# Taking four means over features from the sum of two chunks: the additions on GpSimd and VectorE

## The reference, cut to what matters

```
x = x + a_alpha * attention(gamma * rms(x) + beta)        # 16 heads; rms: x * rsqrt(mean(x*x) + eps)
x = x + f_alpha * swiglu(gamma * rms(x) + beta)           # hidden 1024
h = x * scale * rsqrt(mean(x*x) + eps)                    # MLP with gelu, 8-bit rounding of its hidden values
x = y + x
x = x + up(relu(down(x) + bd)) + bu                       # adapter, width 128, weights made per batch
x = (x - mean(x)) * rsqrt(var(x) + eps) * weight + ...    # layer norm
```

## Time and profile before

| | us |
|---|---|
| median of 3 runs | 1082.66 (1082.04 to 1083.32) |
| the profiled execution | 1081.34 |
| its span, first to last instruction | 1079.5 |
| PE busy | 996.1 |
| DVE busy | 749.6 |
| ACT busy | 552.4 |
| POOL busy | 194.8 |

### The profile page before, as it was taken

The page is one execution under the profiler, slowest core; times in us unless marked ns, Lnnn a source line. Parts: engine busy times, 40 slices in busy tenths (PEclk is TensorE's granted clock), DMA queues, the critical chain, the costliest instruction groups (busy, mean ns, idle before and its releaser), DMA issues.

```text
span 1079.5 us, 22413 instructions
## 1 busy us (share of the span) xinstructions
PE 996.1 (92%) x7426; PEld 846.0 (78%) x7426; DVE 749.6 (69%) x1711; ACT 552.4 (51%) x1160; POOL 194.8 (18%) x250
## 2 busy tenths in 40 slices
PE   5586999999999999999999999999999999998965
PEld 4244769798988979797989889797979898896952
DVE  3735468786777877786867778777868677776552
ACT  3163464656555564646565555646465655545430
POOL 1411421111120202021111202020211112020210
PEclk9576989999999999999999999999999999999995
DMA  8984543040403022130404030221304040300000
GB/s 287 292 326 130 203 148 89 2 138 2 138 1 118 20 74 63 40 98 1 137 1 137 1 117 20 74 63 40 98 1 137 1 137 1 117 13 20 2 20 10
DMA packets 78049, 89.45 MB, mean 83 GB/s; under 512 B 18672, under 2 KB 64640, under 8 KB 75392
## 3 DMA queue, kind: packets, MB, share of 16 engines
q1 hardware_dynamic: 72368, 63.86, 19.9%
q0 software_dynamic: 2304, 16.78, 4.2%
q10 hardware_dynamic: 3344, 8.39, 2.3%
HBM read 63.14 MB, written 25.31 MB: 82 GB/s over the span
## 4 chain that ended last, share of the span: by engine, by line
PE 74%; issue 10%; DVE 5%; DMA 4%; ACT 3%; POOL 2%; SPq 2%; ACTq 0%; DVEq 0%; POOLq 0%
PE bank L648 15%; PE bank L603 14%; PE bank L617 7%; PE bank L572 6%; PE bank L562 5%; PE bank L546 5%; PE bank L520 5%; PE bank L506 3%; PE bank L666 3%; PE bank L529 2%; ACT probs L877 2%; PE bank L680 2%; PE bank L686 1%; PE bank L589 1%; PE bank L627 1%
## 5 line engine op out<-in xcount | busy, mean ns | idle before, releaser
L463 POOL TENSOR_TENSOR act_lo<-act_f,act_hi 128x256 fp32r<-128x256 f32 x128 | 95.9, 755 | 414.4 <-ACT act_hi L920 414.4
L877 ACT ACTIVATE probs<-bank 128x512 f32<-128x512 f32 x256 | 139.6, 599 | 54.7 <-PE bank L562 53.9
L1132 DVE TENSOR_REDUCE neg_max<-bank 128x2 f32<-128x512 f32 x256 | 162.0, 682 | 0.4 <-PE bank L546 0.4
L914 ACT ACTIVATE silu_g<-bank 128x256 f32<-128x256 f32 x128 | 49.2, 385 | 190.2 <-PE bank L603 190.0
L956 ACT ACTIVATE gelu_g<-bank,r 128x256 f32<-128x256 f32 x128 | 60.8, 475 | 95.6 <-PE bank L648 94.8
L562 PE MATMUL bank<-q_stack,k_stack 128*128 128x256 f32 x512 | 98.5, 315 | 12.1 <-ACT probs L877 11.8
L648 PE MATMUL bank<-up_hi,h_hi 128*128 128x256 f32 x512 | 108.1, 293 | 1.6 <-DVE y L1105 1.0
L603 PE MATMUL bank<-h_hi,gh_hi 128*128 128x256 f32 x512 | 103.6, 284 | 4.6 <-DVE h_lo L1193 4.6
L603 PE MATMUL bank<-h_lo,gh_hi 128*128 128x256 f32 x512 | 103.3, 283 | 0.0
L603 PE MATMUL bank<-h_hi,gh_lo 128*128 128x256 f32 x512 | 103.0, 283 | 0.0
L648 PE MATMUL bank<-up_lo,h_hi 128*128 128x256 f32 x512 | 102.9, 282 | 0.0
(11 more groups left out here) (160 smaller groups left out, 2131.8 us busy)
## 6 DMA issues: line engine op xcount, KB each, us to landing
hyper<-w_hyper POOLq DMA_DIRECT2D x16, 1024.0 KB, 6.7
q_stack<-q_dram SPq DMA_DIRECT2D x96, 128.0 KB
k_stack<-k_dram SPq DMA_DIRECT2D x96, 128.0 KB
q_dram<-probs SPq DMA_DIRECT2D x16, 512.0 KB, 2.8
k_dram<-probs SPq DMA_DIRECT2D x16, 512.0 KB, 3.6
x_res<-xT SPq DMA_DIRECT2D x16, 256.0 KB, 2.8
out<-xc SPq DMA_DIRECT2D x16, 256.0 KB, 2.5
x_in<-xT SPq DMA_DIRECT2D x15, 256.0 KB, 2.7
```

The lines of the kernel that those rows point to most:

```text
L463: pool.tensor_tensor(act_lo[:, c % 3, :], act_f[:, c % 2, :], act_hi[:, c % 3, :].bitcast(F32), ALU.subtract).then_inc(g_lo.sem, 1)
L877: act.activation(probs[:, h % SLOTS], halves(SCORE_BANKS[h % 3]), ACT.Exp, scale=float(H / D) ** 0.5).then_inc(s_exp.sem, 1)
L1132: dve.tensor_reduce(neg_max[:, qt, :, pair:pair + 1].rearrange("p a o -> p (a o)"), halves(n % 3), AX_X, ALU.max, negate=True).then_inc(ma ...
```

## The change

Each of the five means but the norm of batches 0 and 1 ahead of attention is now taken of the sum of the two chunks, so the product with mean_w has one chunk. New functions make the sum, in place or in a tile that is free: on GpSimd sum_a (n1, after the sixth act_lo), sum_x and sum_square_x (n4, ahead of layer_out); on VectorE sum_g (n3, between norm_a(nxt) and scaled_y(g)) and sum_f (n2, after residual_1). New semaphores n1_sum to n4_sum tell TensorE. On TensorE project_v(nxt, 1) moves from behind norm_f to ahead of ln_var, and norm_f waits once for the sum in place of once for each chunk. project_v(nxt, 0) for a run without a is dropped; no run has nxt without a.

```diff
+                def sum_a(b):
+                    pool.wait_ge(n1_act.sem, n1_act.at(b, 1))
+                    pool.tensor_tensor(h1[:, 0, :], h1[:, 0, :], h1[:, 1, :], ALU.add).then_inc(n1_sum.sem, 1)
+                def sum_x(b):
+                    pool.wait_ge(x4_dve.sem, x4_dve.at(b))
+                    pool.tensor_tensor(adapt_h[:], x3[:, 0, :], x3[:, 1, :], ALU.add).then_inc(n4_sum.sem, 1)
+                def sum_square_x(b):
+                    pool.wait_ge(n4_act.sem, n4_act.at(b, 1))
+                    pool.tensor_tensor(sq4[:, 0, :], sq4[:, 0, :], sq4[:, 1, :], ALU.add).then_inc(n4_sum.sem, 1)
...
+                            if nxt and c == 5:
+                                sum_a(nxt)
...
+                        sum_x(g)
+                        sum_square_x(g)
                         layer_out(g)
...
+                def mean_of_sum(at, total):
+                    return pe.matmul(at, mean_w[:], total, start=True, stop=True)
...
+                        pe.wait_ge(n1_sum.sem, n1_sum.at(b, back=2))
+                        mean_of_sum(bank[4][:, 0:T], h1[:, 0, :]).then_inc(n1_pe.sem, 1)
...
-                    for c in range(DC):
-                        pe.wait_ge(n2_act.sem, n2_act.at(b, c + 1))
-                        mm = pe.matmul(bank[4][:, 0:T], mean_w[:], h2[:, c, :], start=(c == 0), stop=(c == DC - 1))
-                    mm.then_inc(n2_pe.sem, 1)
+                    pe.wait_ge(n2_sum.sem, n2_sum.at(b))
+                    mean_of_sum(bank[4][:, 0:T], h2[:, 0, :]).then_inc(n2_pe.sem, 1)
...
-                    pe.wait_ge(n3_act.sem, n3_act.at(b, 1))
+                    pe.wait_ge(n3_sum.sem, n3_sum.at(b))
                     for t in range(TT):
-                        for c in range(DC):
-                            mm = pe.matmul(bank[3][:, t:t + 1], sq3[:, c, t * P:(t + 1) * P], mean_w[:, 0:1],
-                                           start=(c == 0), stop=(c == DC - 1))
+                        mm = pe.matmul(bank[3][:, t:t + 1], sq3[:, 0, t * P:(t + 1) * P], mean_w[:, 0:1], start=True, stop=True)
...
-                    pe.wait_ge(x4_dve.sem, x4_dve.at(b))
-                    mean(bank[7][:, 0:T], x3).then_inc(n4_pe.sem, 1)
+                    pe.wait_ge(n4_sum.sem, n4_sum.at(b, 1))
+                    mean_of_sum(bank[7][:, 0:T], adapt_h[:]).then_inc(n4_pe.sem, 1)
...
-                    pe.wait_ge(n4_act.sem, n4_act.at(b, 1))
-                    mean(bank[6][:, 0:T], sq4).then_inc(n4_pe.sem, 1)
+                    pe.wait_ge(n4_sum.sem, n4_sum.at(b, 2))
+                    mean_of_sum(bank[6][:, 0:T], sq4[:, 0, :]).then_inc(n4_pe.sem, 1)
...
-                            norm_a(nxt)
+                            norm_a(nxt, summed=f is not None)
...
+                    if nxt:
+                        project_v(nxt, 1)
                     if g:
                         ln_var(g)
-                    if nxt and not a:
-                        project_v(nxt, 0)
                     if a:
                         norm_f(a)
-                    if nxt:
-                        project_v(nxt, 1)
...
+                def sum_g(b):
+                    dve.wait_ge(n3_act.sem, n3_act.at(b, 1))
+                    dve.tensor_tensor(sq3[:, 0, :], sq3[:, 0, :], sq3[:, 1, :], ALU.add).then_inc(n3_sum.sem, 1)
+                def sum_f(b):
+                    dve.wait_ge(n2_act.sem, n2_act.at(b, DC))
+                    dve.tensor_tensor(h2[:, 0, :], h2[:, 0, :], h2[:, 1, :], ALU.add).then_inc(n2_sum.sem, 1)
...
                     if nxt:
                         norm_a(nxt)
+                    if f:
+                        sum_g(f)
                     if g:
                         scaled_y(g)
...
                         residual_1(a)
+                        sum_f(a)
                     if g:
                         layer_norm(g)
```

More of the change, by code:

```diff
@@ L244, in build @@
         den_act, o_dve = sem("den_act", 4), sem("o_dve", 16)
+        n1_sum, n2_sum, n3_sum, n4_sum = sem("n1_sum"), sem("n2_sum"), sem("n3_sum"), sem("n4_sum", 2)
         wo_mm, x1_dve, x1_bias = sem("wo_mm", DC), sem("x1_dve", 2), sem("x1_bias", DC)
@@ L507, in mean, with norm_a @@
                     return mm
-                def norm_a(b):
+                def mean_of_sum(at, total):
+                    return pe.matmul(at, mean_w[:], total, start=True, stop=True)
+                def norm_a(b, summed=False):
                     pe.wait_ge(n1_act.sem, n1_act.at(b, 1))
-                    mean(bank[4][:, 0:T], h1).then_inc(n1_pe.sem, 1)
+                    if summed:
+                        pe.wait_ge(n1_sum.sem, n1_sum.at(b, back=2))
+                        mean_of_sum(bank[4][:, 0:T], h1[:, 0, :]).then_inc(n1_pe.sem, 1)
+                    else:
+                        mean(bank[4][:, 0:T], h1).then_inc(n1_pe.sem, 1)
                 def project_qk(b):
```

## The result

The changed kernel takes 1100.05 us (median of 4, 1097.32 to 1109.02) against 1082.56 (1082.04 to 1083.32; a fourth execution has joined the three above): ratio 1.0175, 95% interval 1.0117 to 1.0234, slower by 17.5 us. The forecast was 1099. The profiled execution took 1100.66 (span 1098.5). Three executions of the experiments ran in a slow state (two of the eighth at 1869 us, one of the sixth at 1139 us) and are in no ratio.

What follows compares the result with a forecast made beforehand. PE, busy 92%, was taken to set the pace. Thirteen full runs +9.4, end runs +1.4 and +1.1, run 1 +4.4 sum to +16.3 us; on 1081.34 that is 1097.6, with the median 1.3 above, 1099; range 1090 to 1108.

Steps and rivals of the forecast that it cites:

- norm_a, 0.0 us: At norm_a, POOL's sum_a is free, but its gain is hidden because ffn_out waits for act_lo: 0.0 us per full run.
- norm_g, +0.87 us: At norm_g, PE stands 1.3 us for sum_g, queued on DVE behind residual_2 and norm_a: +0.87 us per full run.
- Tail, -0.15 us: From ln_mean to the up projection, sum_f eats ln_mean's gain and gated_u(1) holds the fourth up piece: -0.15 us per run.
- the 0.17 us: In the tail, gated_u(0)'s wait for DVE's Newton steps, which come earlier, is taken out: 0.17 us.
- The stated waits: In the tail: ln_mean waits little or not for POOL, ln_var within 0.3 us; guess_f's wait moves to PE's norm_f.
- The up projection's waits for act_u: Sign in the new profile: PE's waits for gated_u in the up projection grow from 0.2 to about 0.8 us per run.
- Run 1, +4.4 us: Second pipeline run: sum_g queues behind norm_a's two tensor_scalars of 4.64 us; norm_g's next group +3.75, low clock 0.7: +4.4 us.
- Ends: Runs at the pipeline's ends: three pay sum_f's add, 3 x 0.45 = +1.4; run 16 +1.1; the last 0.
- The sum: Whole kernel: full runs 9.4, end runs 1.4 and 1.1, second pipeline run 4.4, together +16.3 us, giving 1099.
- PE's busy time: Sign in the new profile: TensorE's busy time falls by about 30 us, 2.1 us of it in each full run.
- the collision of GpSimd adds with DVE: Rival: sum_x beside normalise(1) holds DVE by one add's length, 0.75 us, in each full run: 1109; chance 0.09.
- the saving stand: Rival: sum_g ready when PE reaches norm_g and up not waiting, so 2.1 us per run stay: 1055 or 1060; chance 0.04.

Runs made afterwards that it cites:

- experiment 8: Changed kernel with sum_g on GpSimd, behind the adapter's base add, in place of VectorE; 1089.55 us, ratio 1.0075 to the kernel before.
- the sixth: Changed kernel with norm_g moved behind attend(a, 0), guess_g behind exps(6), and norm_f as before without sum_f; 1084.86 us, ratio 1.0026.
- experiment 7: Changed kernel with norm_g and norm_f as before; only GpSimd's three sums and the moved project_v stay; 1077.97 us, ratio 0.9962.
- experiment 11: Changed kernel with norm_g, norm_f and norm_a as before; only the layer norm's two sums and the moved project_v stay; 1077.9 us, ratio 0.9969.
- experiment 1: Changed kernel with norm_g as before: eight short matmuls, no sum_g; the other sums stay; 1081.18 us, ratio 0.9994.
- experiment 2: Kernel before with norm_g's sum alone: sum_g on VectorE behind norm_a, norm_g of four matmuls; 1101.08 us, ratio 1.0168.
- experiment 9: Kernel before with norm_g merely moved behind attend(a, 0) and guess_g behind exps(6), still eight matmuls, no sum; 1096.35 us, ratio 1.0152.
- experiment 10: Changed kernel with norm_g and norm_f as before and project_v(nxt, 1) back behind norm_f; 1076.44 us, ratio 0.996.
- run 16: A pipeline run inside every execution, not a follow-up kernel: it has no attention and is serial; forecast +1.1 us.
- experiment 5: Changed kernel with norm_g moved on TensorE behind attend(a, 0), and ScalarE's guess_g behind exps(6) in place of exps(5); 1089.19 us, ratio 1.0072.
- experiment 4: Changed kernel with norm_f as before (two products, each behind its square, no sum_f), moved project_v kept; 1097.66 us, ratio 1.0135.
- experiment 3: Changed kernel with three float32 matmuls of no use put ahead of norm_g's wait for the sum; 1099.11 us, ratio 1.0152.

## Why the prediction was right, and where it was not

- **norm_a, 0.0 us:** right. 0.83 us to ffn_out before and after; with and without sum_a 59.07 us (experiments 7 and 11).
- **norm_g, +0.87 us:** right. Measured +0.86 (5.55 to 6.41), PE idle 1.24 (forecast 1.3), 21.1 us in all (forecast near 20). Experiments 1 and 2 show that this site costs the whole loss, and experiment 8 that DVE's order sets the length of the wait. The step left out the low stretches of the clock that come behind some of the stands.
- **Tail, -0.15 us:** it was 0.0 (+0.01). The term that failed is the 0.17 us which I took as gated_u(0)'s wait for the Newton steps, as the row named it. In the changed kernel these end at 649.90, and gated_u(0) still starts at 650.38, waiting for gelu(0) of 649.71. From gelu(0)'s start to gated_u(0) it is 0.67 us, and it was 0.66 in the kernel before (636.92 to 637.58), so it had hung on the gelu alone there too, which guess_f times. sum_f and the shorter ln_mean cancelled as worked out: guess_f is 5.22 us behind ln_mean, and was 5.17. The stated waits came about: ln_mean did not wait for POOL, nor did ln_var (its sum ended at 645.20, 0.28 us before it), and guess_f waited for PE.
- **The up projection's waits for act_u** were forecast to grow from 0.2 to 0.8 us in a run; they are 0.6 (8.6 us in 15).
- **Run 1, +4.4 us and 0.45 for its tail:** 2.6. sum_g again stood behind the two tensor_scalars that GpSimd holds up (4.66 us), but this stretch of DVE began at 135.32 instead of 137.11, so the group behind norm_g began 1.7 us later against the run's start and not 3.75. The change is not shown to be what brought that stretch forward: the clock, low from before run 1 began, rose at 103.0 in this profile and at 106.8 in that of the kernel before. The low stretch around norm_g was longer, 10.2 us in place of 6.8, with PE waiting in it; how the other 0.9 us divides between it and the forecast 0.45 for sum_f stays open. In the profiles of experiments 1, 7, 9, 10 and 11, where VectorE makes no sum for norm_g, run 1 took anything from 69.0 to 73.1 us, so one profile each does not price it to better than some microseconds.

```profile
135.32 4.66 DVE L1144 TENSOR_SCALAR h<-h,par_a 128x256 f32<-128x256 f32 x2
139.90 0.41 DVE L1118 TENSOR_TENSOR sq<-sq 128x256 f32<-128x256 f32 x1
```

- **Ends:** run 0 +0.3 (0.45 forecast), which says little, as run 0 ends between 97.6 and 104.8 us over the thirteen profiles. Run 15 +2.2 (0.45), mostly low clock: experiments 7 and 11, which differ by sum_a alone, have run 15 at 60.5 us with 6.8 us of low clock and at 58.1 without. Runs 16 and 17 -0.3 (+1.1), where the clock was up for part of the stretch in which it had been low.
- **The sum:** forecast +16.3, the two spans differ by 19.0. The steady runs without the clock make 0.82 x 13 = 10.7 of it (9.4 forecast) and the clock 3.6 that I had not allowed for there; run 1 was forecast too high by 2. That the median came to 1100.05 against 1099 is therefore partly luck, since errors cancel, and the changed kernel's own executions spread by 11.7 us. The 10.7 us of the steady runs are no luck.
- PE's busy time fell by 23 us, not 30. The removed products do take off what I counted, and slightly more (a mean's group went from 1.03 to 0.59 us). But a full run with the clock up lost 1.67 us of busy time and not 2.1, and the three with a low stretch lost 0.2, since the same work is busy for longer there. A part of the difference may be that where PE now stands, the end of its last record is no longer covered by the next; no run separates that.
- The rivals: the collision of GpSimd adds with DVE did not happen (from 614.45 to ln_mean it was 15.03 us before, and 15.02 after from 627.24; the DVE instructions beside sum_x took 0.48 us each, as before), and experiment 1 excludes it. Nor did the saving stand. Experiments 5 and 9 show something neither I nor the rival had: even without the stand, most of norm_g's time on PE is spoken for, since the next scores wait for ACT's exponentials. With norm_g away from its place (experiment 9) scores(5) began 1.15 us after the scores ahead of it instead of 1.58, and 0.27 of these 0.43 us were lost again before attend. By these numbers, as an estimate, even a sum that was ready in time could have saved about 0.2 us there in a run, not 0.46.

## What to carry to other kernels

Taking work off the busiest engine by giving a small operation to a less busy one pays only if two things hold: that engine's queue is free when the input is ready, and the input is ready early enough for the added operation to end before the busiest engine arrives. Look at what is queued in front, not at the busy share, and at when the input comes. An instruction on the busiest engine may be the cover of another engine's chain; before it is halved or moved, find what the next instruction waits for. Make such a change one site at a time: of four sites here (the layer norm's two means count as one), one cost everything, one ate a gain, one did nothing and one, the layer norm's, pays 0.3 to 0.4% (experiments 7, 10 and 11).

## What the runs showed that was not expected

Some stands of 1.24 us, in an otherwise busy TensorE, were followed by 3.4 us at a granted clock of 0.50 (1.2 GHz), from 1.2 to 1.8 us after the start of norm_g, at a cost of 1.1 to 1.5 us each. It happened in 3, 2 and 3 of 13 full runs of the changed kernel and experiments 2 and 4, which all have the stand. It happened in none of the 130 full runs of the ten other profiles: the kernel before, experiment 3, where the stand was filled with matmuls, experiment 8, where it was 0.73 us, and the seven without it. So the low stretches go with the stand. Why they follow some stands and not others, no run shows.

Whether they also widen the spread of the executions is not shown: the changed kernel's four lay 11.7 us apart, those of experiments 2 and 4 3.7 and 4.2. The kernel before, 1.3 us apart in the first four, was 15.5 apart in 17 later ones (5.8 but for one at 1093.20) and 9.4 in 31.
